# A value bias folded into the output bias, and value banks copied by two engines, in a four-layer mixer

## The reference

```python
q = (x @ Wq + bq).reshape(...)
k = (x @ Wk + bk).reshape(...)
v = (x @ Wv + bv).reshape(...)
scores = einsum('bthd,bshd->bhts', q, k) / sqrt(HD) + alibi, causal
attn = softmax(scores, axis=-1)
out = einsum('bhts,bshd->bthd', attn, v)
return out @ Wo + bo
```

## Time and profile before

| | before |
|---|---|
| runs | 2574.23, 2570.89, 2565.89 us |
| median | 2570.89 us |
| profiled execution | 2570.88 us |
| its span, first to last instruction | 2569.1 us |
| mean granted clock of TensorE | 0.929 |
| busy in the span: PE, DVE, ACT, POOL | 83%, 66%, 49%, 30% |

### The profile page before, as it was taken

How to read it: one execution, slowest core, us unless ns; L and a number is a source line. 1 busy time by engine, 2 the same in 40 slices (tenths; PEclk the granted TensorE clock), 3 DMA queues, 4 the chain that set the end, 5 groups by cost and what they waited for, 6 DMA issues and landing times.

```text
span 2569.1 us, 58418 instructions
## 1 busy us (share of the span) xinstructions
PE 2133.7 (83%) x24731; PEld 1219.4 (47%) x24832; DVE 1703.6 (66%) x3811; ACT 1260.4 (49%) x2025; POOL 781.8 (30%) x658
## 2 busy tenths in 40 slices
PE   3558988888797885769789999999999999998964
PEld 1346565655565563334344354444444545444432
DVE  5646475656656455358878788787887878777337
ACT  2414333342424221215666666766667666766723
POOL 2132332414233101162424244243452432412110
PEclk8879999899999987868999999999999999999987
DMA  3201010101001011143323134141331412213063
GB/s 96 66 18 51 18 51 25 59 18 51 20 32 45 7 51 50 50 134 106 92 74 109 43 84 129 45 121 57 84 117 42 117 51 76 76 35 104 30 229 131
DMA packets 131252, 179.28 MB, mean 70 GB/s; under 512 B 8832, under 2 KB 94848, under 8 KB 130992
## 3 DMA queue, kind: packets, MB, share of 16 engines
q1 hardware_dynamic: 128816, 175.02, 22.3%
q10 hardware_dynamic: 2176, 0.52, 0.1%
HBM read 97.40 MB, written 77.59 MB: 68 GB/s over the span
## 4 chain that ended last, share of the span: by engine, by line
PE 62%; DVE 24%; ACT 6%; issue 4%; POOL 2%; DMA 1%; SPq 0%; DVEq 0%; POOLq 0%; ACTq 0%
PE general L882 10%; PE general L573 10%; PE out_of_heads L760 9%; DVE maxima L1408 8%; PE scores L716 6%; PE general L559 4%; PE general L893 4%; PE general L539 3%; PE turned_scores L730 3%; PE out_of_heads L647 3%; PE out_of_heads L657 2%; PE scores L605 2%; PE general L547 2%; DVE probs_turned L1355 1%; PE scores L665 1%
## 5 line engine op out<-in xcount | busy, mean ns | idle before, releaser
L1408 DVE TENSOR_REDUCE maxima<-scores 128x1 f32<-128x512 f32 (+3 forms) x1536 | 793.1, 553 | 237.2 <-PE scores L692 122.9
L1080 ACT ACTIVATE probs_turned<-turned_scores 128x512 f32<-128x512 f32 x1152 | 680.6, 601 | 386.9 <-PE turned_scores L692 203.4
L716 PE MATMUL scores<-k_stacks,q_stacks 59*128 59x512 bf16 (+3 forms) x1536 | 447.4, 338 | 79.5 <-DVE maxima L1408 73.4
L730 PE MATMUL turned_scores<-q_stacks,k_stacks 61*128 61x512 bf16 (+3 forms) x1536 | 438.5, 330 | 2.6 <-ACT probs_turned L1080 2.4
L716 PEld LDWEIGHTS scores<-k_stacks,q_stacks 59*128 59x128 bf16 x1536 | 124.0, 95 | 311.9 <-DVE maxima L1408 247.3
L1716 POOL TENSOR_TENSOR ln_low<-ln 128x512 bf16<-128x512 f32 x128 | 138.3, 1088 | 284.1 <-DVE ln L1390 261.2
L1695 POOL TENSOR_SCALAR ln<-x_for_attention,ln_mean_var,ln_rstd 128x256 f32<-128x256 f32 x104 | 127.9, 1240 | 188.9 <-DVEq L1487 98.4
L1007 ACT ACTIVATE gate_tanhs<-general,feature_vectors 128x512 f32<-128x512 f32 x96 | 66.0, 687 | 204.2 <-PE general L573 200.0
L1631 POOL TENSOR_TENSOR state_low<-state_doubled,state_high 128x2048 bf16<-128x2048 f32 x14 | 57.0, 4068 | 358.8 <-ACT state_high L1013 358.8
L1373 DVE TENSOR_SCALAR reciprocals<-scores 128x16 f32<-128x16 f32 x64 | 11.1, 174 | 226.3 <-PE scores L665 226.3
L760 PE MATMUL out_of_heads<-probs_turned,values_odd_and_heads_out 128*17 128x512 f32 (+3 forms) x1536 | 155.6, 500 | 0.3 <-ACT probs_turned L1080 0.3
(11 more groups left out here) (240 smaller groups left out, 5445.5 us busy)
## 6 DMA issues: line engine op xcount, KB each, us to landing
x_after_attention<-x_residual SPq DMA_DIRECT2D x16, 1024.0 KB, 5.2
x_times_wo<-x_wo_out SPq DMA_DIRECT2D x64, 256.0 KB, 2.1
q_stacks<-q_stack SPq DMA_DIRECT2D x64, 256.0 KB, 4.5
k_stacks<-k_stack SPq DMA_DIRECT2D x64, 256.0 KB, 4.8
x_for_attention<-in_x SPq DMA_DIRECT2D x8, 1024.0 KB, 5.4
x_residual<-in_x SPq DMA_DIRECT2D x8, 1024.0 KB, 5.4
x_for_attention<-x_after_attention SPq DMA_DIRECT2D x8, 1024.0 KB, 5.5
ffn_h<-x_times_wo SPq DMA_DIRECT2D x32, 256.0 KB, 5.9
```

The costliest lines, as they stand in the source:

```text
L716: mx = pe.matmul(bank_s[:, first * P:(first + tiles) * P], QS[at_s:at_s + QROWS, r, i * P:(i + 1) * P], KS[at_s:at_s + QROWS, r, k0 * P:(k ...
L730: ex = pe.matmul(bank_t[:, first * P:(first + tiles) * P], KS[at_t:at_t + KROWS, r, j * P:(j + 1) * P], QS[at_t:at_t + KROWS, r, i0 * P:(i ...
L1080: nc.scalar.activation(PR[:, s % SLOTS, :], TB[s % 2][:, :], ACT.Exp).then_inc(sem["ex_taken"], 1)
L1408: r = dve.tensor_reduce(MP[:, gg % 2, g, at:at + 1], max_bank[m][:, first * P:(first + tiles) * P], AX.X, ALU.max)
```

## The change

1. The value bias is no longer added to the values. Instead `bv @ Wo` is computed once, at the border of the halves, and added to the output bias in `ROW[:, 1]`. For this SyncE loads the bias a second time, by features (`BV`, two DMAs of 128 elements of 4 bytes, each element to its own partition). VectorE spreads it over 128 columns in high and low parts (`split_value_bias`, step 51). TensorE multiplies these by `Wo` (six matmuls of 256 columns, step 52, after waits for the weights and the parts), and VectorE adds the result to the row (`output_bias`, step 53). GpSimd waits for that once before it uses the row.
2. In the second half, of each pair of value banks ScalarE copies bank 0 (one copy of 128x512, at steps 31 and 39, ahead of the step's exponential), and VectorE copies bank 1 (one copy of 128x512), where VectorE had made four additions of 128x256. TensorE and SyncE wait for both engines' semaphores, `v_act2` and `v_ready2`.

```diff
             sp.dma_start(ROW[:, :, :], rows.partition_broadcast(P)).then_inc(sem["const_in"], 16)
+            for k in range(KT):
+                sp.dma_start(BV[:, k:k + 1], rows[0, k * P:(k + 1) * P].rearrange("(p a) -> p a", a=1)
+                             ).then_inc(sem["bv_in"], 16)
...
@@ tensor, values_unit
-                    pe.wait_ge(sem["v_ready2"], 4 * (gg // GROUPS + 1))
+                    for name in ("v_act2", "v_ready2"):
+                        pe.wait_ge(sem[name], 2 * (gg // GROUPS + 1))
...
@@ tensor, loop of the first half
                 fill(1, s // BATCH, s % BATCH)
+                if s == B * BATCH + 52:
+                    pe.wait_ge(sem["w_split"], 8)
+                    pe.wait_ge(sem["bv_split"], 1)
+                    by_token(general_for("dve", "bv_done"), O_, BVT, 0, (0,)).then_inc(sem["g_dve"], 1)
...
@@ tensor, fill_slot
-                        take_bank(bank, consumer)
+                        take_bank(bank, "v_act2" if kind == "v" and bank == 0 else consumer)
...
-                        mm.then_inc(sem["g_act" if engine == "act" else "g_dve"], 1)
-                        general_of[engine].append(G[bank])
+                        taker = "act" if kind == "v" and bank == 0 else engine
+                        mm.then_inc(sem[f"g_{taker}"], 1)
+                        general_of[taker].append(G[bank])
...
@@ scalar, fill_softmax
+                if batch_in(nb) and k in (31, 39):
+                    values_in(nb, 2 * (31, 39).index(k))
                 if batch_in(fb) and k in (5, 9, 33, 37) and (fb or k > 9):
...
+            def values_in(nb, c):
+                if c == 0 and nb >= 2:
+                    act.wait_ge(sem["probs_used"], NU * GROUPS * (nb - 1))
+                nc.scalar.copy(V[nb % 2][:, 2 * c:2 * c + 2, :].rearrange("p n (h v) -> p n h v", v=HV)[:, :, :, 0:HD],
+                               general_in().rearrange("p (n h v) -> p n h v", n=2, v=HD)).then_inc(sem["v_act2"], 1)
...
@@ vector, values_in
-                for n in range(2):
-                    i = dve.tensor_tensor(dst[:, n, :, 0:HD], bank[:, n * D:(n + 1) * D].rearrange(
-                        "p (h v) -> p h v", v=HD), ROW[:, 0, :].rearrange("p (h v) -> p h v", v=HD), ALU.add)
-                i.then_inc(sem["v_ready2"], 1)
+                dve.tensor_copy(V[nb % 2][:, 2 * c:2 * c + 2, :].rearrange("p n (h v) -> p n h v", v=HV)[:, :, :, 0:HD],
+                                general_in().rearrange("p (n h v) -> p n h v", n=2, v=HD)
+                                ).then_inc(sem["v_ready2"], 1)
+
+            def split_value_bias():
+
+                dve.wait_ge(sem["bv_in"], 16 * KT)
+                dve.wait_ge(sem["xt_dve"], KT * (TURNS.index((1, "o", B - 1)) + 1))
+                wide = BV[:, :].rearrange("p (k a) -> p k a", a=1).broadcast_to([P, KT, P])
+                step(dve.tensor_copy(BVT[0], wide))
+                dve.tensor_tensor(BVT[1], wide, BVT[0], ALU.subtract).then_inc(sem["bv_split"], 1)
+
+            def output_bias():
+
+                step(dve.tensor_tensor(ROW[:, 1, :], general_in()[:, 0:D], ROW[:, 1, :], ALU.add))
+                dve.sem_inc(sem["bv_done"], 1)
...
@@ vector, take_banks
                     if k in (31, 39):
-                        for n in range(2):
-                            values_in(nb, 2 * (31, 39).index(k) + n)
+                        values_in(nb, 2 * (31, 39).index(k) + 1)
...
@@ vector, loop of the first half (the weights are split at k == 50)
+                if b == B and k == 51:
+                    split_value_bias()
+                if b == B and k == 53:
+                    output_bias()
...
@@ gpsimd
+                    if b == 0:
+                        pool.wait_ge(sem["bv_done"], 1)
```

More of the change, by code:

```diff
@@ L201, in mixer_kernel @@
         ROW = sb("row_vectors", [P, 3, D], F32)
+        BV = sb("value_bias_by_feature", [P, KT], F32)
         ident = sb("identity", [P, P], BF16)
@@ L236, in mixer_kernel @@
         U = XI[:, :, :].rearrange("p a b -> p (a b)")
+        BVT = [OL[:, n:n + 1, :].rearrange("p n (k t) -> p (n k) t", k=KT) for n in range(2)]
         HM = flat(OL[:, :, :]).rearrange("p (s t) -> p s t", s=2)
@@ L433, in free_for_final @@
                     sp.wait_ge(sem["pk_raw2"], 8 * B)
[L434 removed]
+                    for name in ("v_act2", "v_ready2"):
+                        sp.wait_ge(sem[name], 2 * B)
                 elif b == 3:
```

7 lines of the change are left out of this document (2 added, 5 removed).

## The result

| | kernel before | changed kernel |
|---|---|---|
| median of 9 runs each (lowest to highest) | 2570.5 us (2563.9 to 2574.8) | 2561.4 us (2557.6 to 2565.1) |
| ratio of the two | | 0.9972 (0.9962 to 0.9982) |
| the same pair, measured again in another set | 2568.1 us (31 runs) | 2559.7 us (8 runs), 0.9970 (0.9957 to 0.9983) |
| profiled execution, span | 2570.88, 2569.1 us | 2558.81, 2557.0 us |
| mean granted clock of TensorE | 0.929 | 0.934 |

The forecast was 2570.2, the range 2564.0 to 2577.5.

What follows compares the result with a forecast made beforehand. TensorE held 62% and VectorE 24% of the chain, with VectorE the limit around the second half's bias additions. Terms -8.7 + 2.8 + 4.4 + 0.8 = -0.7 us from 2570.9 gave 2570.2 us, range 2564.0 to 2577.5.

Steps and rivals of the forecast that it cites:

- What bounds the kernel: Whole kernel: chain is TensorE for 62%, VectorE for 24%; a VectorE saving counts only where VectorE holds the chain.
- the steady term: Six batches of the second half: paired copies save 0.72 us in each of 12 groups; term -8.7 us (-9.6 to -6.0).
- ScalarE takes the path: Second half: ScalarE's copy delays exponentials and so TensorE, the 8.7 is lost; 2578.9 us, chance 0.09.
- half the gain goes: Steady groups: TensorE takes both banks together, late ScalarE leaves only VectorE's share, half of 8.7; 2574.5 us, chance 0.10.
- the one of the lead-in: Maxima at 1141.7 to 1175: TensorE's clock stays high, VectorE becomes the limit; 2564.3 us (2562 to 2566), chance 0.11.
- The batch before the six: Second half, batch where VectorE idles between its two groups: the two groups give about 0.1 us.
- First batch: Second half's start: ScalarE's copy waits behind two tanh, so VectorE's first maxima come at 1141.37 instead of 1138.61, +2.8 us.
- Border: Between the halves: bias split and six matmuls delay the transposes and first product by 4.4 us (+4.2 to +5.1).
- the rival given 0.12: Border: clock rises earlier as products and transposes run together, half-speed products shrink to none; -2.6 us, 2567.6 us.
- Start: Kernel start: two small bias DMAs ahead of masks and key rows in SyncE's queue delay the rest, +0.8 us (0 to 1.3).
- The base: Starting time of the sum: profiled execution of the kernel before, 2570.88 us, with the median of three runs 2570.89.
- the four terms: Copies in pairs -8.7, first batch +2.8, border +4.4, start +0.8 us; sum -0.7 us.

Runs made afterwards that it cites:

- e9: Kernel before, unchanged, profiled and timed a second time against itself: ratio 1.0005, mean 2568.6 us.
- e1: Kernel before plus only the two bias loads and the border work, its result written to an unread spare row: ratio 0.9998, mean 2568.0 us.
- e3: Changed kernel, but VectorE copies both banks in the first batch: ratio 0.9963 to the kernel before, mean 2558.5 us.
- e15: Changed kernel with the border's split, six products and addition each done twice: ratio 0.9957 to the kernel before, mean 2556.1 us.
- e16: Changed kernel with the two bias loads moved behind the first weights' loads: ratio 0.9956 to the kernel before, mean 2555.9 us.
- e7: Changed kernel without bias work (value bias left out), VectorE copying both banks in the first two batches: ratio 0.9933 to the kernel before, mean 2551.2 us.
- e12: Changed kernel with late loads, border work at TensorE step 67, VectorE copying both banks in the first two batches: ratio 0.9962 to the kernel before.

## Why the prediction was wrong

- **What bounds the kernel, and the steady term: right.** 12 x 0.72 = 8.6 us forecast for the twelve groups, 12 steps of 0.72 or 0.73 found (8.7), copies of 0.68 and 0.58, no exponential that became a bound. The rivals in which ScalarE takes the path, or half the gain goes, have nothing in the traces. Nor has the one of the lead-in: the granted clock of the 34 us of maxima is 0.50 in the changed kernel (1146.8 to 1181.0) as it was before.
- **The batch before the six: 0.1 forecast, 1.1 found.** The step that failed is the reading of the earlier trace rows as "VectorE idles, so it gains nothing". The idle time is a wait for TensorE, which had itself waited for the bank.
- **First batch: +2.8 forecast; +2.2 and +2.5 in the changed kernel's two traces, 0.9 against the additions by the means over traces, none in the time.** The chain was right in each step (second block at 1138.42 forecast 1138.39, first maxima 1141.53 forecast 1141.37, although the half had begun 0.8 later). The step that failed is what it was set against: first maxima at 1138.61 in one execution of the kernel before, taken as fixed. They stand behind VectorE's own small instructions, and e9 starts them 2.2 us later against the border with no edit at all, because two of these took 1.00 and 1.97 us.
- **Border: +4.4 forecast, 2.0 to 2.3 in the changed kernel's two traces, and this is not the forecast mechanism.** The split took 0.29 and 0.42 as worked out (0.30 and 0.42). The step that failed is "I assume that this stretch only moves": the clock rose at 1027.4 instead of 1032.4, so the second transposes took 1.16 for sixteen, the first product came 3.6 us later and not 4.4, and the products took 0.11 each, which gave back 2.6 by the 48th and left 1.0. That is the mechanism of the rival given 0.12 (-2.6), and not by chance: in all six traces with the work at step 52 (the changed kernel's two, e1, e3, e15, e16) the first eleven products start within 1.09 us, in the twelve others, with it moved or without it, within 2.08 or 2.09. I had it in the text, six products and the transposes run together, and gave it too little. That the rival's sum (+1.8) is so near to the 2.0 to 2.3 is in part luck: it overlooked the 0.7 us of the transposes, and 1.0 to 1.2 came from the longer half-clock interval near 1073, which no term had.
- **Start: +0.8 forecast, +1.2 and +0.8 in the two traces.** Nearly right. The Trainium skill, page "DMA: Bandwidth & Descriptors", section "Bandwidth", with its floor of 0.68 us (given there for 4 KB issued from GpSimd), made an estimated 1.4 of it. The two issues took 1.06 together here, and the key rows' issue came 1.1 us later: the measurement lies between.
- **The base: 2570.9 taken, 2568.0 right.** The sum started from one execution, and the median of three runs agreed with it. The 101 later runs of the same kernel have set means of 2567.2 to 2568.6 and a mean of 2568.0. This alone is 2.9 us.
- **The clock between the places: nothing forecast, an estimated 1.7.** The changed kernel's sets had 344 and 348 us of half clock, the kernel before 350 to 356; 7 us less at 0.24 is 1.7. Some of these 7 us may be the border's, which its term has already.

With these in place of the forecast's terms: 2568.0 - 8.7 - 1.1 + 0.9 + 2.1 + 1.0 - 1.7 = 2560.5, where 2561.4 and 2559.7 were measured. This sum was made with the result known, from means over few traces and the clock's line, so its closeness proves no single term. The bounds written at the four terms give 2567.0 to 2576.7; nothing in them reaches the result. The range was too narrow below because each small cost that I added on the slow side had a bound for itself, and the base and the clock had none.

## What to carry to other kernels

A saving that is repeated in steady groups can be read from one trace to a hundredth of a microsecond, and here it carried the result. A cost that occurs once, of 1 to 3 us, can't: it needs the base and the affected stretch from several executions before it is netted against the saving, and it has to be followed instruction by instruction: one number for the border (+2.0) held two causes. And idle time of an engine in front of an instruction is no cover as long as the engine that it waits for is waiting for the instruction that gets shorter.

## What the runs showed of the hardware that I had not expected

- TensorE's granted clock differs between executions of one program in mid-stretch: three intervals at the 1.2 GHz level within 75 us in one execution, none of them in the next, at 0.7 to 1.2 us of the schedule each, with the same instructions.
- 1 us more at the half clock goes with only 0.24 us of the kernel's time (233 executions). That VectorE holds much of the chain would explain it; no run tests this.
- In five traces (e9, e1, e3, e7, e12) a small VectorE instruction that takes 0.17 us otherwise took 0.9 to 2.0 us: it had started while a GpSimd cast or subtraction of 128x1024 ran, and ended 0.02 us behind it. It stood directly ahead of the first maxima.
- More work for TensorE at the border made the stretch after it faster: with the six products ahead of the transposes the next products ran at 0.11 us each instead of 0.21 from their first on, and the 3.6 us by which the first of them was late became 1.0 by the 48th.
- Two tiny loads at the head of a queue shift the start by 0.7 to 1.5 us, differing between executions of one kernel (1.2 and 0.8).
